# Decoder layer with mLSTM and routed experts: router by column groups ahead of the second projection, clears in the first turn, first feed-forward pair ahead of the last mLSTM transposes

## Chip, cores, metric

One core of a Trainium2 chip (trn2). The metric is the device time of one execution in microseconds, the median of several runs. All arithmetic is fp32 (TensorE operands too; some are split into an fp32r high and low part).

## What is computed

The input x is 16 sequences of 256 tokens with 512 features, beside a context of the same shape. Cut to what matters:

```python
x = layernorm(x + attention(x))            # 16 heads of 32, 4 key/value heads, rope on half of each head
x = layernorm(x + mlstm(q=x, k=ctx, v=ctx))  # 16 heads; two gates per head from [x, ctx, ctx]
logits = x @ router_w.T                    # 512 -> 16 experts
top2 = top_k(logits + router_bias, 2)      # weights: softmax scores of the two, made to sum to 1
out = sum over the two of weight * (silu(x @ Wu[e]) * (x @ Wg[e])) @ Wd[e]
out += (silu(x @ Su) * (x @ Sg)) @ Sd      # the shared expert, hidden width 512
return layernorm(x + out)
```

## The kernel before

`attention_and_mlstm` makes everything up to the router and the shared expert, one sequence (256 tokens, two tiles of 128) per turn; `experts` then runs 79 tiles of routed tokens, and `finish` normalises. The change touches the first function only.

**A turn is software-pipelined over three sequences**: `body(b, y, w, more)` holds attention of sequence b, the mLSTM of y=b-1, and router and shared expert of w=b-2. The turns are (0, -, -), (1, 0, -), then b=2 to 15 with all three, then (-, 15, 14) and (-, -, 15); b=3 to 14 are a hardware loop on VectorE and b=2 to 14 on the others. Each engine has its own instruction stream, written out by hand in an order of its own; the order between engines is set by semaphores alone (`wait(engine, signal, turn, count)`). Nothing is planned by a program.

**TensorE's order in a steady turn**: `qkv(0)`; transposes of x2 of w (`turn(x2T_ready, x2, 4)`, PSUM banks 4 and 5); transposes of x1 of y (banks 6 and 7); `qkv(1)` (L1111, 16 instructions for 8 matmuls, since an fp32 matmul is issued as two); `route()` (L1142: for both token tiles 4 matmuls that accumulate over the feature chunks, stationary x2T 128x128, moving router weights 128x16); `gate_mm()` (L1126, 24 matmuls of 256 columns); `ug(0)` of the shared expert (L1174, eight matmuls, su then sg); `turn_qk()` (L1161); `ug(1)`, `rank` (L1149 and L1150, which count the tokens chosen per expert), `ug(2)`, `ug(3)`; then the mLSTM's decay, score and sum matmuls over 16 heads with the scores of attention between them, then attention's second half, `down`, and the output projection (L1401). `ug(c)` for c of 2 and more waits for `hT_done` of pair c-2, which `hidden(c-2)` on VectorE gives (L865 and L870, behind `tanh(c-2)` on ScalarE, L571).

**ScalarE's order** there: `pass_through(0)` (L564), copy of x2T from PSUM (L578), x1T_hi (L583), `pass_through(1)`, Exp (L589) and Ln (L591) of the gates with a table load each time the function changes, qkT_hi (L597 and L600; this tile is also x1T_hi, so it waits for `mq_in`, the transfers that read it), then the tanh steps.

**VectorE's order**: `rope(0)`, x1T_lo (L926), `rope(1)` (L718 to L726), the router's top 2 (L935 to L947, small steps, each waiting for the one before), the gates (L955, then L957, which releases Exp, then L958), qkT_lo (L961 and L964), `hidden(0)`, two gate steps, `hidden(1)`, and so on.

**GpSimd's order**: `centre(y)` (L457 to L465), then, released by `gates_ready`, ctxT_hi (L488) and ctxT_lo (L490) of the next sequence, the key stack's 12 transfers, the routed ids' indirect transfers, and the stores. `clear_rows()` (four transfers that fill the id table and the spare rows, some 2.5 MB) comes between turn 0 and turn 1.

**SyncE** issues transfers: `mq_stack` from x1T (12), the next xT, `q_stack` from qkT (8 hi rows, 4 lo rows), the maxima, and `mk_stack` (12); at the start the constants (`first`), and after turn 0's maxima the six `late` loads, router weights and shared expert weights.

```python
def wait(eng, signal, b, n, rest=None):      # n-th step of turn b
def run(eng, body, then=None):               # the turns, in order
X_hi, X_lo = cast to fp32r, X - X_hi         # "hi" and "lo" rows of the stacks
```

Of the kernel before, what the change touches and what calls it, by code (L numbers as in the profile page):

```python
# [13 lines left out]
ALU = mybir.AluOpType  # L14
# [108 lines left out]
def attention_and_mlstm(nc, block, x, xT, ctx_in, ctxT, wqkv, wo, gate_w, gate_b, ln_scale, router_w, router_b,  # L123
# [3 lines left out]
    with ExitStack() as ctx:  # L127
# [23 lines left out]
        rw_sb = sb("rw_sb", [P, KC, E])  # L151
# [21 lines left out]
        mask_sb = arden[:, 0:P]  # L173
        ones_k = sb("ones_k", [P, HD])
# [76 lines left out]
        ps = ctx.enter_context(nc.psum_tensor("ps", [P, 8, 512], F32))  # L251
        ranks_of_turn = ps[:, 0, 0:2 * ST * E]
# [54 lines left out]
        lg_ready, lg_done = sig("lg_ready", 1), sig("lg_done", 1)  # L307
        top_step, choice_done = sig("top_step", 5 + TOPK), sig("choice_done", 1)
# [51 lines left out]
        def _(sp):  # L360
# [4 lines left out]
            late = [(rw_sb[:, :, :], router_w), (rb_sb[:, :], router_b.partition_broadcast(P)),  # L365
# [5 lines left out]
            sp.wait_ge(consts.sem, 1)  # L371
# [3 lines left out]
            def body(b, y, w, more):  # L375
# [9 lines left out]
                if b is not None:  # L385
# [3 lines left out]
                    wait(sp, qk_lo_done, b, 2)  # L389
                    stack(sp, q_stack, qkT_hi, qkT_lo, None, q_in, (None, None, "lo"))  # L390
                    if y is None:
                        sp.wait_ge(first_in.sem, 11 * 16)
                        sp.dma_start(wo_sb[:, :, :], wo).then_inc(first_in.sem, 16)
# [18 lines left out]
        def _(pool):  # L412
            rest = (pool.alloc_register("rest"), consts.sem)
            nc.gpsimd.memset(gb_sb[:, :], 0.0).then_inc(consts.sem, 1)
            nc.gpsimd.memset(one_col[:, :, :], 0.0).then_inc(fills.sem, 1)
# [52 lines left out]
            def body(b, y, w, more):  # L468
# [9 lines left out]
                if b is not None:  # L478
                    if y is None:
                        send_keys()  # L480
# [28 lines left out]
                if b is not None:  # L509
                    if y is not None:  # L510
                        wait(pool, av2_pair, y, PAIRS, rest=rest)
                    pool.dma_start(ctx_sb[:, :, :, :].rearrange("p t h d -> p t (h d)"), one(ctx_v, b)).then_inc(ctx_row_in.sem, 16)
                if y is not None:
# [23 lines left out]
            clear_rows()  # L537
# [10 lines left out]
        def _(act):  # L548
# [5 lines left out]
            def body(b, y, w, more):  # L554
# [24 lines left out]
                if y is not None:  # L579
# [3 lines left out]
                    nc.scalar.copy(x1T_hi[:, :, :], ps[:, 6:8, :].rearrange("p a (c s) -> p (a c) s", s=S))\  # L583
                        .then_inc(x1T_hi_done.sem, 1)
                if b is not None:
                    pass_through(1)
# [5 lines left out]
                if b is not None:  # L592
# [7 lines left out]
                    nc.scalar.copy(qkT_hi[:, KC, :], ps[:, 4, 0:S]).then_inc(qk_hi_done.sem, 1)  # L600
                def exp_gap():
# [88 lines left out]
        def _(dve):  # L690
# [4 lines left out]
            nc.vector.tensor_tensor(head_sel[:, :], id_sb[:, 0:H], id_sb[:, H:GR], ALU.add).then_inc(gwlo.sem, 1)  # L695
            nc.vector.tensor_reduce(is_lo[:, :], id_sb[0:GR, H:GR], AX.X, ALU.add).then_inc(gwlo.sem, 1)
# [1114 lines left out]
```

## Time and profile before

| | |
|---|---|
| median of 3 runs | 2015.57 us (2010.05 to 2018.85) |
| profiled execution, its own time | 2011.49 us |
| its span | 2009.9 us |
| mean granted TensorE clock | 0.962 of full |
| TensorE (PE) busy | 1834.2 us, 91% |
| VectorE (DVE) busy | 1141.7 us, 57% |
| GpSimd (POOL) busy | 690.4 us, 34% |
| ScalarE (ACT) busy | 644.1 us, 32% |
| chain that ended last | PE 78%, DVE 11%, issue 4%, ACT 3%, DMA 2% |

The sequences take the first 1475 us or so, the experts most of the rest. A busy TensorE need not be one at its peak: the times of its instructions include the pipeline's length, so their distance from start to start tells more than their duration.

### The profile page before, as it was taken

To read this page: it belongs to the slowest core of one execution; us is meant where nothing else is said; L and a number is where in the kernel's file an instruction comes from. 1 tells how busy PE (TensorE), PEld (TensorE's weight loads), DVE (VectorE), ACT (ScalarE), POOL (GpSimd) and SP (SyncE) were. 2 spreads that over 40 slices of the span, in tenths; PEclk is the share of its full clock that TensorE was granted. 3 is DMA by queue.
4 is the path that set the end of the run, shared out by engine and by line. 5 is a ranking of instruction groups with operands and counts; after the bars stand their busy time and mean duration, and the time that the engine had idled before them with its cause. 6 is when DMAs were issued, how large, how long until landed. Compare 5 with 4: busy or idle time off the path is not lost.

```text
span 2009.9 us, 35358 instructions
## 1 busy us (share of the span) xinstructions
PE 1834.2 (91%) x10992; PEld 1175.2 (58%) x10993; DVE 1141.7 (57%) x2407; ACT 644.1 (32%) x1355; POOL 690.4 (34%) x752
## 2 busy tenths in 40 slices
PE   5779999999999999999999999999789999999990
PEld 3456575766757676675766657576444544444440
DVE  3457776777677677766767677676432222222225
ACT  0242433424234252433434233352312211221124
POOL 3214233342323424233343323322224444444440
PEclk7889999999999999999999999998899999999995
DMA  5644243443424344242444424332416577656549
GB/s 160 190 112 113 58 109 83 102 118 69 123 63 102 103 94 127 49 123 74 98 112 89 123 63 102 90 79 73 147 43 134 109 202 168 120 119 145 92 76 342
DMA packets 151420, 225.94 MB, mean 112 GB/s; under 512 B 31888, under 2 KB 106640, under 8 KB 148816
## 3 DMA queue, kind: packets, MB, share of 16 engines
q1 hardware_dynamic: 102048, 132.94, 25.3%
q0 software_dynamic: 38112, 91.86, 20.2%
q10 hardware_dynamic: 11216, 0.61, 0.4%
q8 instruction: 22, 0.36, 0.1%
q14 instruction: 22, 0.18, 0.0%
HBM read 94.44 MB, written 48.57 MB: 71 GB/s over the span
## 4 chain that ended last, share of the span: by engine, by line
PE 78%; DVE 11%; issue 4%; ACT 3%; DMA 2%; SPq 1%; POOL 1%; DVEq 0%; ACTq 0%; POOLq 0%
PE ps L1621 14%; PE ps L1174 11%; PE ps L1111 8%; PE ps L1640 7%; PE ps L1401 6%; PE ps L1376 5%; PE ps L1260 5%; PE ps L1296 3%; PE ps L1365 3%; PE ps L1243 3%; DVE arden L912 3%; DVE smax L894 3%; PE ps L1126 2%; PE ps L1222 2%; PE ps L1609 2%
## 5 line engine op out<-in xcount | busy, mean ns | idle before, releaser
L1621 PE MATMUL ps<-ug_w,rowsT 128*128 x632 | 289.2, 601 | 7.9 <-SPq L1470 4.5
L502 POOL DMA_INDIRECT routed_ids<-pair_w,pos_w x64 | 64.0, 1000 | 446.3 <-DVE pair_w L790 431.7
L1621 PEld LDWEIGHTS ps<-ug_w,rowsT 128*128 128x128 f32 x632 | 121.4, 193 | 161.7 <-issue 161.7
L1510 POOL DMA_INDIRECT sum_rows<-y_sb,pairs x79 | 125.7, 1591 | 245.4 <-DVE y_sb L1588 126.6
L1111 PE MATMUL ps<-wqkv_sb,xT_sb 128*128 128x256 f32 (+1 forms) x512 | 172.6, 491 | 5.8 <-DMA wqkv_sb<-in_wqkv 5.8
L912 DVE RECIPROCAL arden<-ps 128x256 f32<-128x256 f32 x64 | 112.4, 1757 | 114.2 <-PE ps L1365 111.0
L1576 DVE SCALAR_TENSOR_TENSOR silu<-tanh,ps 128x256 f32<-128x256 f32 x79 | 33.2, 421 | 249.4 <-ACT tanh L1531 249.4
L1004 DVE SCALAR_TENSOR_TENSOR weighted<-ps,decay 128x384 f32<-128x384 f32 x256 | 140.2, 553 | 60.7 <-PE ps L1243 51.5
L894 DVE TENSOR_REDUCE smax<-ps 128x2 f32<-128x512 f32 x256 | 163.6, 680 | 13.4 <-PE ps L1296 13.4
L647 ACT ACTIVATE decay<-ps,g_col 128x256 f32<-128x256 f32 x256 | 121.3, 474 | 136.5 <-PE ps L1224 98.9
L1531 ACT ACTIVATE tanh<-ps 128x256 f32<-128x256 f32 x79 | 30.3, 384 | 370.7 <-PE ps L1621 370.7
L1640 PE MATMUL ps<-d_w,hidT 128*128 x316 | 148.6, 593 | 0.1
L668 ACT ACTIVATE probs<-ps 128x1024 f32<-128x1024 f32 x128 | 126.3, 1027 | 58.3 <-PE ps L1345 57.7
L1111 PEld LDWEIGHTS ps<-wqkv_sb,xT_sb 128*128 128x128 f32 x512 | 96.7, 192 | 80.5 <-issue 73.5
L1296 PE MATMUL ps<-k_stack,q_stack 96*128 96x256 f32 x512 | 112.8, 325 | 29.1 <-DMA q_stack<-qkT_lo 12.9
L564 ACT COPY hid_sq<-ps 128x320 f32<-128x320 f32 x32 | 13.6, 425 | 385.4 <-PE ps L1111 385.4
L1174 PE MATMUL ps<-x2T,su_sb 128*128 128x256 f32 x512 | 124.6, 387 | 1.9 <-DVE hT L870 1.6
L1401 PE MATMUL ps<-wo_sb,hid_sq 128*128 128x512 f32 x256 | 116.1, 607 | 5.5 <-DVE hid_sq L914 5.5
L1174 PE MATMUL ps<-x2T,sg_sb 128*128 128x256 f32 x512 | 121.0, 379 | 0.0
L515 POOL TENSOR_TENSOR hvar<-hvar,eps_half 128x32 f32<-128x32 f32 x16 | 87.4, 5464 | 87.2 <-DVE hvar L887 81.9
L1376 PE MATMUL ps<-sd_sb,hT 128*128 128x512 f32 x256 | 114.0, 598 | 0.7 <-DVE hT L870 0.7
L1260 PE MATMUL ps<-weighted,ctx_sb 128*32 128x256 f32 (+1 forms) x1024 | 108.6, 333 | 5.9 <-issue 5.5
(253 smaller groups left out, 3600.2 us busy)
## 6 DMA issues: line engine op xcount, KB each, us to landing
q_stack<-qkT_hi SPq DMA_DIRECT2D x128, 128.0 KB, 3.7
mk_stack<-ctxT_hi SPq DMA_DIRECT2D x128, 128.0 KB
mq_stack<-qkT_hi SPq DMA_DIRECT2D x128, 128.0 KB, 2.4
ug_w<-in_expert_ug SPq DMA_DIRECT2D x16, 1024.0 KB, 5.9
xT_sb<-in_xT SPq DMA_DIRECT2D x16, 512.0 KB, 3.4
q_stack<-qkT_lo SPq DMA_DIRECT2D x64, 128.0 KB, 4.9
x_sb<-in_x POOLq DMA_DIRECT2D x16, 512.0 KB, 3.9
ctxT_sb<-in_ctxT POOLq DMA_DIRECT2D x16, 512.0 KB, 3.8
```

Of the source, the lines that this page charges most:

```text
L668: nc.scalar.activation(probs[:, i % 4, :, :, :].rearrange("p j t s -> p (j t s)"), ps[:, 2 * (i % 2):2 * (i % 2) + 2, :].rearrange("p j n ...
L894: nc.vector.tensor_reduce(smax[:, k, :], ps[:, 3 + 4 * (k % 2), :].rearrange("p (t s) -> p t s", s=S), AX.X, ALU.max).then_inc(smax_done.s ...
L912: nc.vector.reciprocal(arden[:, :], ps[:, 6 + c % 2, cols]).then_inc(arden_done.sem, 1)
L1004: nc.vector.scalar_tensor_tensor(weighted[:, h % 4, :], ps[:, qk2_bank(h), 0:384], SCALE, decay[:, h % 2, :], ALU.mult, ALU.mult).then_inc ...
L1111: ins = nc.tensor.matmul(ps[:, 2 * t + lo // 512, 0:hi - lo], xT_sb[:, c, P * t:P * t + P], wqkv_sb[:, c, lo:hi], start=c == 0, stop=c == ...
L1174: ins = nc.tensor.matmul(ps[:, 6 + c % 2, lo:lo + S], wt[:, k, P * c:P * c + P], x2T[:, k, :], start=k == 0, stop=k == KC - 1)
L1260: nc.tensor.matmul(ps[lo:lo + HD, 4 + i // 4, col + cols.start:col + cols.stop], ctx_sb[:, t, h, :], weighted[:, h % 4, part], start=t == ...
L1296: ins = nc.tensor.matmul(ps[:, 3 + 4 * (k % 2), S * t:S * t + S], q_stack[0:96, k, P * t:P * t + P], k_stack[0:96, k // GQ, :], start=True ...
L1376: ins = nc.tensor.matmul(ps[:, 2 + t, :], hT[:, c, P * t:P * t + P], sd_sb[:, c, :], start=c == 0, stop=c == SC - 1)
L1401: ins = nc.tensor.matmul(ps[:, 6 + t, :], attT[:, c, P * t:P * t + P], wo_sb[:, c, :], start=c == 0, stop=c == KC - 1)
L1621: ins = nc.tensor.matmul(ps[:, 2 + k % 2, :], rowsT[:, k % 2, c, :], ug_w[:, bass.ds(slot, 1), c, :].rearrange("p o n -> p (o n)"), start= ...
L1640: ins = nc.tensor.matmul(ps[:, 4 + k % 2, :], hidT[:, k % 2, f, :], d_w[:, bass.ds(slot, 1), f, :].rearrange("p o d -> p (o d)"), start=f ...
```

## The change

1. **Router.** `route()` is split. `route_chunks()`, right ahead of `qkv(1)`, multiplies each chunk of router weights (128x32: 16 columns and 16 of zeros, hence a memset of rw_sb on GpSimd) as stationary with x2T's chunk as moving operand (256 columns), each chunk into its own 32 partitions of PSUM bank 4. ScalarE copies the 128x256 result to SBUF (into `arden`'s place). Behind `qkv(1)`, `route()` adds the four groups and transposes in one step: per token tile one matmul with the copied tile as stationary and `chunk_sum` (128x16) as moving operand. `route_chunks` waits for `x2T_done` before `qkv(1)`; before, that wait stood behind it.
2. **Clears.** `clear_rows()` moves into turn 0, behind the load of ctx_sb, and waits for the late loads first.
3. **First turn's stacks.** The key stack's hi rows go out as soon as hi is there, before lo; the query stack's lo rows go out from ScalarE's queue and not SyncE's.
4. **Turn (-, 15, 14).** `route_chunks()` and `ug(0)` come ahead of the transposes of x1, which go to banks 2 and 3 there.

```diff
-        rw_sb = sb("rw_sb", [P, KC, E])
+        rw_sb = sb("rw_sb", [P, KC, HD])
+        chunk_sum = sb("chunk_sum", [P, E])
+        lgT_sb = arden
+        X1_AT, X1_AT_LAST = 6, 2
...
 sync:
-            sp.wait_ge(consts.sem, 1)
+            sp.wait_ge(consts.sem, 2)
...
-                    wait(sp, qk_lo_done, b, 2)
-                    stack(sp, q_stack, qkT_hi, qkT_lo, None, q_in, (None, None, "lo"))
-                    if y is None:
+                    if y is not None:
+                        wait(sp, qk_lo_done, b, 2)
+                        stack(sp, q_stack, qkT_hi, qkT_lo, None, q_in, (None, None, "lo"))
+                    else:
...
 gpsimd:
+            nc.gpsimd.memset(rw_sb[:, :, :], 0.0).then_inc(consts.sem, 1)
...
                     if y is None:
-                        send_keys()
+                        wait(pool, qk_hi_done, b, 2)
+                        stack(pool, k_stack, qkT_hi, qkT_lo, KC, k_in, ("hi", None, "hi"))
+                        wait(pool, qk_lo_done, b, 2)
+                        stack(pool, k_stack, qkT_hi, qkT_lo, KC, k_in, (None, "lo", None))
...
                     pool.dma_start(ctx_sb[:, :, :, :].rearrange("p t h d -> p t (h d)"), one(ctx_v, b)).then_inc(ctx_row_in.sem, 16)
+                    if y is None:
+                        pool.wait_ge(late_in.sem, 6 * 16)
+                        clear_rows()
...
             body(0, None, None, True)
-            clear_rows()
             body(1, 0, None, True)
...
 scalar:
-                    nc.scalar.copy(x1T_hi[:, :, :], ps[:, 6:8, :].rearrange("p a (c s) -> p (a c) s", s=S))\
+                    at = X1_AT if b is not None else X1_AT_LAST
+                    nc.scalar.copy(x1T_hi[:, :, :], ps[:, at:at + 2, :].rearrange("p a (c s) -> p (a c) s", s=S))\
                         .then_inc(x1T_hi_done.sem, 1)
+                if w is not None:
+                    wait(act, lgT_ready, w, 1)
+                    nc.scalar.copy(lgT_sb[:, :], ps[:, 4, 0:S]).then_inc(lgT_done.sem, 1)
...
+                    if y is None:
+                        wait(act, qk_lo_done, b, 2)
+                        stack(act, q_stack, qkT_hi, qkT_lo, None, q_in, (None, None, "lo"))
...
 vector:
+            nc.vector.tensor_reduce(chunk_sum[:, :], id_sb[:, :].rearrange("p (j n) -> p n j", n=HD)[:, 0:E, :], AX.X, ALU.add)\
+                .then_inc(gwlo.sem, 1)
...
-                        lg = ps[:, 4, 0:ST * E].rearrange("p (t e) -> p t e", e=E)
+                        lg = ps[:, 4, S:S + ST * E].rearrange("p (t e) -> p t e", e=E)
...
 tensor:
+                def route_chunks():
+                    wait(pe, x2T_done, w, 1)
+                    for c in range(KC):
+                        ins = nc.tensor.matmul(ps[HD * c:HD * c + HD, 4, 0:S], rw_sb[:, c, :], x2T[:, c, :], start=True, stop=True)
+                    ins.then_inc(lgT_ready.sem, 1)
+
                 def route():
-                    wait(pe, x2T_done, w, 1)
+                    wait(pe, lgT_done, w, 1)
                     for t in range(ST):
-                        for c in range(KC):
-                            ins = nc.tensor.matmul(ps[:, 4, E * t:E * t + E], x2T[:, c, P * t:P * t + P], rw_sb[:, c, :],
-                                                   start=c == 0, stop=c == KC - 1)
+                        ins = nc.tensor.matmul(ps[:, 4, S + E * t:S + E * t + E], lgT_sb[:, P * t:P * t + P], chunk_sum[:, :],
+                                               start=True, stop=True)
...
+                ahead = b is None and y is not None
+                if ahead:
+                    route_chunks()
+                    wait(pe, h_done, y, 1)
+                    ug(0)
                 if y is not None:
                     wait(pe, x1_done, y, ST)
-                    turn(x1T_ready, x1, 6)
+                    turn(x1T_ready, x1, X1_AT_LAST if ahead else X1_AT)
+                if w is not None and not ahead:
+                    route_chunks()
...
-                if w is not None:
+                if w is not None and not ahead:
                     ug(0)
```

The counts of the semaphores consts and gwlo that others wait for grow by one each, and VectorE's x1T_lo reads the banks that x1T_hi reads.

## Rows read from the trace of the kernel before

**Rows 1.** TensorE in a steady turn, in order of time (start us, us, engine, line, operation).

```profile
432.03 5.33 PE L1111 MATMUL ps<-wqkv_sb,xT_sb 128*128 128x512 f32 x16
437.19 1.85 PE L1142 MATMUL ps<-rw_sb,x2T 128*128 128x16 f32 x16
438.90 0.31 PE L1126 MATMUL ps<-qkT_hi,gw_hi 128*64 128x256 f32 x1
...
441.75 1.89 PE L1174 MATMUL ps<-x2T,su_sb 128*128 128x256 f32 x8
...
449.89 0.39 PE L1150 MATMUL ps<-biased,ones_k 128*128 128x32 f32 x2
450.30 1.99 PE L1174 MATMUL ps<-x2T,su_sb 128*128 128x256 f32 x8
```

**Rows 2.** VectorE in the same turn, in order of time.

```profile
438.02 0.49 DVE L718 TENSOR_TENSOR hid_sq<-ps,cos_sb 128x320 f32<-128x320 f32 x1 [3.39 <-ACT v_sb L565]
...
441.43 0.49 DVE L944 TENSOR_TENSOR onehot<-choice,iota_sb 128x32 f32<-128x32 f32 x2
442.02 0.19 DVE L947 TENSOR_TENSOR biased<-onehot 128x32 f32<-128x32 f32 x1
...
442.63 0.92 DVE L957 SCALAR_TENSOR_TENSOR probs<-probs 32x256 f32<-32x256 f32 x1
443.48 2.43 DVE L958 TENSOR_SCALAR probs<-probs 32x256 f32<-32x256 f32 x1
...
449.82 0.42 DVE L870 SCALAR_TENSOR_TENSOR hT<-gate_sb,ps 128x256 f32<-128x256 f32 x1
```

**Rows 3.** ScalarE in the same turn; in brackets the idle time before and its end.

```profile
431.36 1.01 ACT L578 COPY x2T<-ps 128x1024 f32<-128x1024 f32 x1
...
446.35 1.01 ACT L597 CAST qkT_hi<-ps 128x1024 fp32r<-128x1024 f32 x1 [0.62 <-PE ps L1161]
```

**Rows 4.** Groups by line: TensorE's column-group form (busy us, mean ns, idle before).

```profile
L1365 PE MATMUL ps<-probs,v_sb 128*32 128x256 f32 x1024 | 81.2, 389 | 2.5 <-DVE hid_sq L914 1.2 <-ACT probs L668 0.4
```

**Rows 5.** GpSimd in the same steady turn, in order of time.

```profile
442.24 1.04 POOL L488 CAST ctxT_hi<-ctxT_sb 128x1024 fp32r<-128x1024 f32 x1 [3.00 <-PE ps L1126]
443.36 2.40 POOL L490 TENSOR_TENSOR ctxT_lo<-ctxT_sb,ctxT_hi 128x1024 fp32r<-128x1024 f32 x1
```

**Rows 6.** One line's instructions over all turns: ns least/median/most.

```profile
L957 DVE SCALAR_TENSOR_TENSOR probs<-probs x16: 414/924/1093, 95.0 to 1394.2; 32x256 f32<-32x256 f32 x16
...
L958 DVE TENSOR_SCALAR probs<-probs x16: 274/2431/2435, 95.8 to 1394.5; 32x256 f32<-32x256 f32 x16
```

**Rows 7.** TensorE behind idle times, in order of time, several stretches.

```profile
35.29 1.22 PE L1296 MATMUL ps<-k_stack,q_stack 96*128 96x256 f32 x4 [12.94 <-DMA q_stack<-qkT_lo]
...
71.59 3.68 PE L1401 MATMUL ps<-wo_sb,hid_sq 128*128 128x512 f32 x4 [2.93 <-DVE hid_sq L914]
...
156.86 8.83 PE L1401 MATMUL ps<-wo_sb,hid_sq 128*128 128x512 f32 x16 [2.61 <-DVE hid_sq L914]
...
1384.00 1.97 PE L1134 MATMUL ps<-id_sb,x 128*128 128x128 f32 x8 [4.83 <-DVE x L920]
...
1646.32 3.69 PE L1621 MATMUL ps<-ug_w,rowsT 128*128 x8 [2.23 <-SPq L1470]
```

**Rows 8.** SyncE's issues in turn 0, turn 1 and a steady turn.

```profile
53.38 0.43 SPq L401 DMA_DIRECT2D sd_sb<-in_sd  x1
...
88.94 9.29 SPq L354 DMA_DIRECT2D mq_stack<-qkT_hi  x8
...
434.81 5.11 SPq L354 DMA_DIRECT2D mq_stack<-qkT_hi  x8
```

**Rows 9.** ScalarE in turn 1.

```profile
106.05 1.01 ACT L597 CAST qkT_hi<-ps 128x1024 fp32r<-128x1024 f32 x1 [7.99 <-issue]
```

**Rows 10.** GpSimd at the end of turn 0.

```profile
82.67 0.56 POOL L530 TENSOR_SCALAR rstd<-mv 128x2 f32<-128x2 f32 x1 [35.37 <-DVE mv L1074]
```

**Rows 11.** Transfer issues by line (count, KB each, median us from issue to landing).

```profile
sd_sb<-in_sd SPq DMA_DIRECT2D x1, 1024.0 KB, 13.1
```

More of the change, by code:

```diff
@@ L307, in attention_and_mlstm @@
         lg_ready, lg_done = sig("lg_ready", 1), sig("lg_done", 1)
+        lgT_ready, lgT_done = sig("lgT_ready", 1), sig("lgT_done", 1)
         top_step, choice_done = sig("top_step", 5 + TOPK), sig("choice_done", 1)
@@ L364, in _ @@
                      (gb_sb[GR:GR + H, :], gate_b[1]), (gb_sb[GR + H:2 * GR, :], gate_b[1])]
-            late = [(rw_sb[:, :, :], router_w), (rb_sb[:, :], router_b.partition_broadcast(P)),
+            late = [(rw_sb[:, :, 0:E], router_w), (rb_sb[:, :], router_b.partition_broadcast(P)),
                     (lns_sb[:, :], ln_scale.partition_broadcast(P)),
@@ L699, in _ @@
             nc.vector.tensor_scalar(filled[:, :], iota_sb[:, 0:E], float(N), None, ALU.mult).then_inc(gwlo.sem, 1)
-            dve.wait_ge(gwlo.sem, 7)
+            dve.wait_ge(gwlo.sem, 8)
             nc.vector.tensor_scalar(row_p[:, :], row_p[:, :], -1.0, float(P - 1), ALU.mult, ALU.add).then_inc(gwlo.sem, 1)
             nc.vector.tensor_scalar(lo_sign[:, :], is_lo[:, :], 2.0, -1.0, ALU.mult, ALU.add).then_inc(gwlo.sem, 1)
-            dve.wait_ge(gwlo.sem, 9)
+            dve.wait_ge(gwlo.sem, 10)
             for t in range(ST):
                 nc.vector.tensor_scalar(token_f[:, t:t + 1], row_p[:, :], float(P * t), None, ALU.add).then_inc(gwlo.sem, 1)
-            dve.wait_ge(gwlo.sem, 11)
+            dve.wait_ge(gwlo.sem, 12)
             dve.wait_ge(pro.sem, 2 + GQ)
@@ L925, in front @@
                         wait(dve, x1T_hi_done, y, 1)
-                        nc.vector.tensor_tensor(x1T_lo[:, :, :], ps[:, 6:8, :].rearrange("p a (c s) -> p (a c) s", s=S),
+                        at = X1_AT if b is not None else X1_AT_LAST
+                        nc.vector.tensor_tensor(x1T_lo[:, :, :], ps[:, at:at + 2, :].rearrange("p a (c s) -> p (a c) s", s=S),
                                                 x1T_hi[:, :, :].bitcast(F32), ALU.subtract).then_inc(x1T_lo_done.sem, 1)
@@ L1119, in gate_mm @@
                     if w is None:
-                        pe.wait_ge(gwlo.sem, 12)
+                        pe.wait_ge(gwlo.sem, 13)
                         pe.wait_ge(late_in.sem, 6 * 16)
@@ L1199, in body @@
                         pe.wait_ge(first_in.sem, 11 * 16)
-                        pe.wait_ge(consts.sem, 3)
+                        pe.wait_ge(consts.sem, 4)
                     turn_qk()
```

## Prediction

> **What bounds it now.** The page has TensorE as by far the busiest engine, so the question is what each part does to the moments at which TensorE starts. I followed one steady turn (b=5) engine by engine; fourteen turns repeat it (b=2 to 15; two of them are written out around the loop, with somewhat shorter gaps between VectorE's small steps). Let T be 432.03, the start of the second projection, and Q be 437.19, its end, where the router starts [rows 1]. TensorE seems to run without a gap up to the rank matmuls, which end at 449.89+0.39=450.28. But ug(2) starts at 450.30, and what releases it is hT of pair 0, written by VectorE at 449.82+0.42=450.24 [rows 1, 2]. So **in each turn ug(2) is already tied to a second chain**, not to TensorE's amount of work. Read backwards it is: hidden(0) <- tanh(0) <- a table load <- the cast of qkT_hi (L597, 446.35) <- Ln <- another table load <- Exp <- VectorE's L957. In VectorE's order the router's top 2 and rope(1) stand in front of L957, and rope(1) begins at 438.02=Q+0.83 [rows 2, 3]. The one slack is the 0.62 us for which ScalarE waits for TensorE's transposes before L597 [rows 3].
>
> **The router in column groups (14 turns).** Removed: 16 instructions, 437.19 to 438.90, 1.71 us [rows 1]. Added:
> - Ahead of the projection a wait for x2T. ScalarE's copy ends at 431.36+1.01=432.37 [rows 3], TensorE is there at T; with some 0.03 for the signal 0.37 us. The whole projection is queued behind it.
> - Eight instructions of 256 columns in four 32-column groups. The same form in the attention sums has 81.2 us for 1024 instructions, 0.079 each beside its neighbours [rows 4]; 8x0.079=0.63 is the upper end. At four at once against the pace of ug's eight (1.89 [rows 1]) they take 1.89/4=0.47, which I take.
> - Behind the projection four instructions with the same 128x128 loads as the removed ones: 4x1.71/16=0.43. ScalarE's added copy (128x256) lies under the projection's 5.16 us, and would cost its own length without it.
>
> TensorE's own sum is 0.37+0.47+0.43-1.71=-0.44 us a turn. But the projection now ends at Q'=Q+0.84, everything on the second chain moves with it, and the gate matmuls end 1.71-0.43=1.28 us nearer to Q'.
>
> **What that triggers on GpSimd.** GpSimd casts ctxT (L488) when the gate matmuls are done, Q+5.05 to Q+6.09, then subtracts (L490), Q+6.17 to Q+8.57 [rows 5]. VectorE's L957 takes 0.41 at its least and 0.92 here: it ends at 443.55, 0.27 behind L488's end. L958 takes 0.27 at its least and 2.43 here, to 445.91, 0.15 behind L490's end [rows 2, 5, 6]. Both stand still until the GpSimd instruction is over; today the long one falls on L958, for which nobody hurries. After the change L488 runs from Q'+3.77 to 4.81 and L490 from Q'+4.89 to 7.29. VectorE is where it was against Q': the two L944 at +4.24 and about +4.5, L947 at +4.83, L957 at +5.44 [rows 2]. **L490 now falls on the critical ones.** The first L944 waits for L488; the second, or L947, meets L490 and waits to Q'+7.3; L957 follows 0.61 behind L947 as today and ends at Q'+8.3 to 8.7, against Q+6.36. Lower bound: L957 alone is held, 7.29+0.27=7.56, +1.20. Upper: +2.39. I take +2.10 in the twelve looped turns (L957 is the nearest row: the same partner, two operands in SBUF) and +1.2 in the two others, where the small steps come earlier. Less the slack of 0.62, ug(2) starts 0.84+2.10-0.62=2.32 us later than today, or 1.42. Nothing behind gives it back: hidden(2) and with it the decay matmuls hang on ug(2). Sum 12x2.32+2x1.42=**+30.7 us**; bounds 14x1.42=20 and 14x2.61=37.
>
> A rule bears on the race between the second L944 and L490. The Trainium skill (SBUF — State Buffer, "SBUF: two separate sides") says that whichever of the two starts first keeps the shared ports for its whole instruction. By that rule a second L944 that starts in the gap before L490 passes, L947 is held in its place, and the sum is some 12x0.25=3 us lower. The rows show the lock, but not who wins a start this close.
>
> **The clock.** Rank's matmuls would end at about Q'+11.8, ug(2) starts at Q'+14.6: TensorE idles 2.8 us in each turn. Behind 2.93 us of idling four L1401 took 3.68; behind 2.61 sixteen took 8.83, where the projection's pace (5.16 for the equal of twelve) gives 6.9, so 1.9 lost; that is the pace of 1.2 in place of 2.4 GHz for a while. Behind 2.23 eight matmuls took 3.69, with nothing lost to see [rows 1, 7]. A gap of 2.8 is nearest the first two but will come in varied phases: I take two turns in three at 1.75, 14x2/3x1.75=**+16.3 us**; bounds 0 and 14x1.9=27.
>
> **First turn.** The stacks' hi rows go out without waiting for lo, and q's lo rows by ScalarE's queue. The first scores start at 35.29, after 12.94 us of waiting for q's lo rows [rows 7]. SyncE issues 8 transfers in place of 12 (5.11/8=0.64 each [rows 8]), 2.6 less, but GpSimd's twelve key transfers are then the last to land: **-2.1**, bounds 0 and -2.6. ScalarE is idle there. One more memset ahead of SyncE's constants and one small reduction lie beside its earlier issues and the first loads; uncovered, under 1 us.
>
> **Clears.** In turn 1 eight mq_stack transfers take 9.29 us against 5.11 in a steady turn, beside the clears, and L597 waits 7.99 us, to 106.05, for the stack to have read its source [rows 8, 9]. With the clears gone twelve go out in 7.7 us from 88.94 and land some 2.4 later, at 99.1: **-6.9**; bounds 0 (the contention has another source) and -8. In turn 0 GpSimd now waits for the late weights, with rstd1 queued behind it. It is idle for 35.37 us up to 82.67 [rows 10]; the last of the weights is issued at 53.38 and lands 13.1 later, at 66.5 [rows 8, 11], and four issues follow. Hidden; if the weights came past 80, the delay would be direct.
>
> **Last two turns.** TensorE waits 4.83 us for x1 [rows 7]. ug(0), some 3.5 us (twice rows 1's eight), now runs in it, and the half pace behind it (1.97 for the eight transposes) goes: **-4.0**, bounds -3.4 and -6. In the very last turn the shorter router gives **-0.7**, bounds 0 and -1.7.
>
> **Sum.** 30.7+16.3-2.1-6.9-4.0-0.7=+33.3. The profiled execution took 2011.5 us (span 2009.9), 0.2% under the median of 2015.6; 2011.5+33.3=2045. What can be told from no change is about 0.5%, 10 us.
>
> **Rivals.**
> - *The lock bites at L957 only, the clock stays up*: 20-14=+6, 2018. For: the small steps move only 32 elements, and a gap of 1.9 us is below the 2.23 that cost nothing. Against: their operands lie as L957's. 0.14.
> - *No collision, faster.* The place is L957's start. If L488 starts at least 1.1 us later than the gates' end lets it (released by something else than the row's TensorE wait), L490 falls on L958 again: 14x(0.84-0.62)-14=-11, 2001. If ug(2) was tied to TensorE alone after all, -0.44x14-14=-20, 1991. For: the release is inferred. Against: the row names the gate matmuls. 0.13 together.
> - *Worst bounds*: 37+27-10=+54, 2066. 0.06.
> - *The groups don't run together* (the change doesn't do what it says): 1.72 in place of 0.47, 14x1.25=17 more, 2062. 0.02; rows 4 speak against it. The Trainium skill (TensorE: Matmul & The Clock Gate, "Part 3: Packing small matmuls") has weight loads overlap running matmuls only where the row group differs; here all share one. By that rule this rival is the truth; the trace disagrees.
>
> **Numbers.** The forecast keeps 0.65, with a range of its own from 2026 (little of the clock's term) to 2062. The range 2010 to 2062 leaves out the fast case and the worst. Slower than 2025.6: 0.71; within 0.5%: 0.17; faster: 0.12.
>
> **What would show it.** Right: in steady turns a wait of TensorE for L870's hT of 2.5 to 3 us, where none is listed; L944 or L947 stretched past 1.5 us; L958 back near 0.27; a granted clock below 1.00 in steady turns; the chunks in 0.43 to 0.63; L597's wait in turn 1 down from 7.99 to about 1; x1's 4.83 gone. Wrong: L957 ending before Q'+7, or ug(2) no later than T+18.3.

## The result, and the profile after

The changed kernel takes **2068.02 us** (median of 4 runs, 2059.82 to 2074.11) against 2016.89 us for the kernel before, run beside it on the same chip (4 runs). The ratio is **1.0257, with an interval of 1.0210 to 1.0304**. The forecast was 2045 us with a range of 2010 to 2062: the direction was right, the size too small, and the median lies outside the range.

The profiled execution took 2059.82 us: a span of 2058.3 us at a mean granted clock of 0.954, against 2009.9 at 0.962. All that follows compares these two spans, so there are 48.4 us to find where the forecast had 33.3. The first lines of the page after, with the chain that ended last:

```profile
span 2058.3 us, 35249 instructions
...
PE 1844.8 (90%) x10928; PEld 1168.2 (57%) x10929; DVE 1144.1 (56%) x2408; ACT 647.2 (31%) x1371; POOL 689.4 (33%) x753
...
PE 68%; DVE 16%; ACT 7%; issue 5%; DMA 2%; SPq 1%; POOL 1%; DVEq 0%; ACTq 0%; POOLq 0%
```

Hardly any engine has more work. What changed is the chain: TensorE's share fell from 78% to 68%, VectorE's rose from 11% to 16% and ScalarE's from 3% to 7%. TensorE's list of waits says where the chain now leaves TensorE (engine, line, what it waited for: us in total, times, longest):

```profile
PE ps L1200 <- DVE hT L890: 43.4, 16, 2.9
PE ps L1329 <- DMA q_stack<-qkT_hi: 15.2, 1, 15.2
...
PE ps L1342 <- DVE probs L1001: 8.4, 1, 8.4
```

The wait of ug(2) for VectorE's hT was not listed for steady turns before; now it comes in all fourteen of them, 2.90 or 2.91 us in the twelve looped ones and 2.4 in the two written out. Here is one steady turn. The numbers of the lines have moved: L1132, L1147, L1187, L1200, L963, L965, L968, L978, L979, L890, L612, L497 and L499 are what L1111, L1126, L1161, L1174, L942, L944, L947, L957, L958, L870, L597, L488 and L490 were. TensorE in order of time, to be laid beside [rows 1]:

```profile
1070.18 0.64 PE L1162 MATMUL ps<-x2T,rw_sb 128*32 128x256 f32 x8 [0.23 <-ACT x2T L589]
1070.75 5.43 PE L1132 MATMUL ps<-wqkv_sb,xT_sb 128*128 128x512 f32 x16
1076.01 0.52 PE L1168 MATMUL ps<-chunk_sum,arden 128*128 128x16 f32 x4
1076.38 0.31 PE L1147 MATMUL ps<-qkT_hi,gw_hi 128*64 128x256 f32 x1
...
1087.33 0.39 PE L1176 MATMUL ps<-biased,ones_k 128*128 128x32 f32 x2
1090.62 3.78 PE L1200 MATMUL ps<-x2T,su_sb 128*128 128x256 f32 x8 [2.91 <-DVE hT L890]
```

Q' is 1076.01. From the first of the eight chunk instructions to the projection behind them it is 0.57 us, and the join takes 0.37. Rank's matmuls are over at 1087.72, ug(2) starts at 1090.62, Q'+14.61, and its eight instructions take 3.78 us instead of 1.89: they run at 1.2 GHz, not 2.4. VectorE in the same turn, beside [rows 2]:

```profile
1079.88 0.86 DVE L963 CAST choice<-top8i 128x4 f32<-128x4 uint32 x1
1080.85 2.65 DVE L965 TENSOR_TENSOR onehot<-choice,iota_sb 128x32 f32<-128x32 f32 x2
1083.61 0.19 DVE L968 TENSOR_TENSOR biased<-onehot 128x32 f32<-128x32 f32 x1
...
1084.22 0.41 DVE L978 SCALAR_TENSOR_TENSOR probs<-probs 32x256 f32<-32x256 f32 x1
1084.56 0.27 DVE L979 TENSOR_SCALAR probs<-probs 32x256 f32<-32x256 f32 x1
...
1090.15 0.42 DVE L890 SCALAR_TENSOR_TENSOR hT<-gate_sb,ps 128x256 f32<-128x256 f32 x1
```

And GpSimd, beside [rows 5]:

```profile
1079.68 1.04 POOL L497 CAST ctxT_hi<-ctxT_sb 128x1024 fp32r<-128x1024 f32 x1 [2.70 <-PE ps L1147]
1080.80 2.36 POOL L499 TENSOR_TENSOR ctxT_lo<-ctxT_sb,ctxT_hi 128x1024 fp32r<-128x1024 f32 x1
```

Put the ends side by side. The cast of four numbers per partition, L963, ends at 1080.74, right after GpSimd's cast ends at 1080.72. L965 is issued at 1080.85, 0.05 us behind the start of GpSimd's subtraction; the two L965 take 2.65 us together instead of 0.49, and the first of them ends only when the subtraction is over (1083.16). L978 and L979, which were stretched before [rows 6], are now at their least, 0.41 and 0.27. So GpSimd's long instruction has moved from an instruction that nobody waits for to one at the head of the critical chain. Over all turns it shows in the duration of these lines (ns least/median/most). L965 stands there twice a turn and only one of the two is held, so its median is the free one; L979 is now free in nearly every turn:

```profile
L965 DVE TENSOR_TENSOR onehot<-choice,iota_sb x32: 191/193/2356, 176.0 to 1503.6; 128x32 f32<-128x32 f32 x32
```

```profile
L979 DVE TENSOR_SCALAR probs<-probs x16: 274/274/2419, 96.5 to 1442.7; 32x256 f32<-32x256 f32 x16
```

The clock, by turn (window, its length, then busy time of each engine, granted clock, DMA share, GB/s). The three rows are a turn with one fall, one without, and one of the late ones:

```profile
432.13:523.15 91.02, 85.06 (x596) 58.03 (x595) 61.51 (x128) 32.65 (x69) 29.58 (x35) 0.98 0.38 92
523.15:612.47 89.32, 83.38 (x596) 56.83 (x595) 61.51 (x128) 32.64 (x68) 29.57 (x35) 1.00 0.40 92
...
1069.12:1161.23 92.11, 86.14 (x596) 58.81 (x595) 61.45 (x128) 32.64 (x68) 29.57 (x35) 0.96 0.37 89
```

and a turn of the kernel before in the same view:

```profile
431.36:518.05 86.69, 83.86 (x600) 58.00 (x599) 61.33 (x128) 32.47 (x68) 29.67 (x35) 1.00 0.41 96
```

So a looped turn costs 89.3 us where the clock stays at 2.4 GHz, 2.63 more than before. With a part of it at 1.2 GHz it is 91.0 (granted clock 0.98) or 92.1 (0.96). Five of the fourteen stay at full clock, two looped ones and the last lose some 1.7 us each, and six in a row, from 793 us on, lose 2.8 each. The two prices come from two lengths of the slow stretch, here one of each (windows set to its ends):

```profile
454.72:458.15 3.43, 3.43 (x10) 2.72 (x9) 2.26 (x5) 0.00 (x0) 3.43 (x8) 0.50 0.94 214
905.29:912.12 6.83, 5.76 (x14) 4.60 (x15) 4.10 (x9) 0.49 (x2) 5.93 (x12) 0.50 0.99 213
```

In the first the granted clock is at half for 3.43 us, all of them behind the start of ug(2) at 453.70; half of that is the 1.7 us. In the second it is at half for 6.83 us and already from 1.07 us before ug(2) starts; TensorE works in 5.76 of them, and half of those is the 2.8.

### The profile page after: what moved, and what is told of

It reads as the page before. It is cut to its first block, busy times and chain, and to the rows that moved or that the text cites. A ratio compares the mean times of both kernels' runs of the same rounds, so it can differ in the third digit from the quotient of the medians.

```text
span 2058.3 us, 35249 instructions
## 1 busy us (share of the span) xinstructions
PE 1844.8 (90%) x10928; PEld 1168.2 (57%) x10929; DVE 1144.1 (56%) x2408; ACT 647.2 (31%) x1371; POOL 689.4 (33%) x753
## 4 chain that ended last, share of the span: by engine, by line
PE 68%; DVE 16%; ACT 7%; issue 5%; DMA 2%; SPq 1%; POOL 1%; DVEq 0%; ACTq 0%; POOLq 0%
PE ps L1654 13%; PE ps L1132 8%; PE ps L1200 7%; PE ps L1673 7%; PE ps L1434 5%; PE ps L1409 5%; PE ps L1293 4%; PE ps L1329 3%; PE ps L1398 3%; DVE arden L932 3%; PE ps L1276 3%; DVE smax L914 3%; PE ps L1255 2%; DVE onehot L965 2%; PE ps L1642 2%
## 5 line engine op out<-in xcount | busy, mean ns | idle before, releaser
L1132 PE MATMUL ps<-wqkv_sb,xT_sb 128*128 128x256 f32 (+1 forms) x512 | 174.4, 494 | 5.9 <-DMA wqkv_sb<-in_wqkv 5.9
L1200 PE MATMUL ps<-x2T,su_sb 128*128 128x256 f32 x512 | 140.1, 422 | 43.4 <-DVE hT L890 43.4
L1609 DVE SCALAR_TENSOR_TENSOR silu<-tanh,ps 128x256 f32<-128x256 f32 x79 | 33.3, 421 | 250.0 <-ACT tanh L1564 250.0
L1132 PEld LDWEIGHTS ps<-wqkv_sb,xT_sb 128*128 128x128 f32 x512 | 96.8, 192 | 86.6 <-issue 79.1
L1200 PEld LDWEIGHTS ps<-x2T,su_sb 128*128 128x128 f32 x512 | 103.7, 210 | 60.5 <-DVE hT L890 45.8
L1200 PE MATMUL ps<-x2T,sg_sb 128*128 128x256 f32 x512 | 130.1, 400 | 0.0
L1200 PEld LDWEIGHTS ps<-x2T,sg_sb 128*128 128x128 f32 x512 | 105.3, 206 | 17.1
```

The source lines that it names most:

```text
L1132: ins = nc.tensor.matmul(ps[:, 2 * t + lo // 512, 0:hi - lo], xT_sb[:, c, P * t:P * t + P], wqkv_sb[:, c, lo:hi], start=c == 0, stop=c == ...
L1200: ins = nc.tensor.matmul(ps[:, 6 + c % 2, lo:lo + S], wt[:, k, P * c:P * c + P], x2T[:, k, :], start=k == 0, stop=k == KC - 1)
```

## The experiments

The theory (T): the release of GpSimd's casts by the gate matmuls comes 1.3 us nearer to Q', so its subtraction holds VectorE's top-2 steps and with them hT; the 2.9 us for which TensorE then waits let its clock fall. Rivals: the router's new work or its new wait costs the time by itself; another part of the change does; the clock's fall has a source of its own. All kernels were timed against the kernel before on their own chip: the first four below on one, the delayed gate matmuls and the old router with later casts on a second, the three parts and the last version on a third. Between chips, and against the changed kernel's own 2068.02, the ratios are the fairer measure. Each kernel has one trace, so what is read from a trace is one execution.

### Starting GpSimd's casts later

```diff
 gpsimd, in the changed kernel, ahead of the cast of ctxT (L497):
                         wait(pool, gates_ready, y, 1)
+                        wait(pool, gabs_done, y, 1)
```

> The changed kernel with one wait more: GpSimd starts the two ctxT instructions (L488 and L490 of before) only when VectorE's L957 (|forget gate|) is done. Port theory: L957 then ends near Q'+5.8 instead of Q'+8.6, the wait for hT ahead of ug(2), 2.9 us in each steady turn, shrinks under 0.3 us, the clock stays at 2.4 GHz in the steady turns, and the time is about 2007 us (before 2017, less 9 of the first and last turns, about 0 in the steady ones). Rival, the chain is long for another reason (rope moved back, ScalarE's extra copy): the wait stays near 2 to 3 us and the time near 2068.

Measured: **1999.27 us** (1998.57 to 2002.41), before 2011.83, ratio 0.9943 [0.9926, 0.9960]. One wait more, on an engine that is a third busy, takes 69 us off the changed kernel by the medians (63 by the two ratios; the kernel before ran 5 us slower on the changed kernel's chip). The expectation was 2007: 5 us of the miss are the chip's, since it reckoned from 2017, and 4 come from the fourteen turns, which are shorter than those of the kernel before (1203.4 us together against 1207.5) where nothing had been expected. VectorE in a steady turn of it (all numbers of lines are one higher):

```profile
954.92 0.17 DVE L964 CAST choice<-top8i 128x4 f32<-128x4 uint32 x1
955.19 0.49 DVE L966 TENSOR_TENSOR onehot<-choice,iota_sb 128x32 f32<-128x32 f32 x2
...
956.40 0.41 DVE L979 SCALAR_TENSOR_TENSOR probs<-probs 32x256 f32<-32x256 f32 x1
956.74 0.27 DVE L980 TENSOR_SCALAR probs<-probs 32x256 f32<-32x256 f32 x1
...
962.33 0.42 DVE L891 SCALAR_TENSOR_TENSOR hT<-gate_sb,ps 128x256 f32<-128x256 f32 x1
```

GpSimd's cast there, and behind it TensorE around ug(2):

```profile
957.17 1.04 POOL L498 CAST ctxT_hi<-ctxT_sb 128x1024 fp32r<-128x1024 f32 x1 [5.13 <-DVE probs L979]
958.29 2.36 POOL L500 TENSOR_TENSOR ctxT_lo<-ctxT_sb,ctxT_hi 128x1024 fp32r<-128x1024 f32 x1
```

```profile
962.37 0.39 PE L1177 MATMUL ps<-biased,ones_k 128*128 128x32 f32 x2
962.80 1.99 PE L1201 MATMUL ps<-x2T,su_sb 128*128 128x256 f32 x8
```

Nothing on VectorE is held any more, L979 ends 5.8 us behind the second projection's end as expected, ug(2) follows rank with no wait listed, and the turn takes 86.42 us at full clock:

```profile
512.08:598.50 86.42, 83.31 (x596) 56.74 (x595) 58.64 (x128) 32.65 (x69) 29.64 (x35) 1.00 0.43 96
```

### The old router in the changed kernel

```diff
 tensor:
-                def route_chunks(): ...
                 def route():
-                    wait(pe, lgT_done, w, 1)
+                    wait(pe, x2T_done, w, 1)
                     for t in range(ST):
+                        for c in range(KC):   # the sixteen instructions of before
 scalar:
-                    nc.scalar.copy(lgT_sb[:, :], ps[:, 4, 0:S]).then_inc(lgT_done.sem, 1)
```

> The changed kernel with the old router (8 accumulating matmuls behind the second projection, no copy on ScalarE); clears, first stacks and the early ug(0) stay. If all of the loss is the router's: 2017-9=2008, steady turns back at 86.7 us. If one of the other parts also costs: above 2020.

Measured: 2001.64 us (2000.36 to 2003.59), ratio 0.9948 [0.9931, 0.9965]. Clears, stacks and the ug pair ahead are thus worth about 10 us together, and everything that the change costs is in the router. The 2008 expected reckoned from 2017 as well.

### The new router alone

```diff
 the changed kernel, router as changed; back to before:
+            clear_rows()   # behind body(0, None, None, True)
+                        send_keys()
-                ahead = b is None and y is not None
+                ahead = False
-        X1_AT, X1_AT_LAST = 6, 2
+        X1_AT, X1_AT_LAST = 6, 6
```

> The router's part alone: clears, first stacks and the turn (-, 15, 14) as before. If the parts add up: the changed kernel's 2068 plus the 9 us that the other parts gave, 2077. If the other parts gave nothing, 2068.

Measured: **2078.19 us** (2072.90 to 2086.52), ratio 1.0335 [1.0301, 1.0369]. As expected (2077), the router costs 66 us by itself, and in company the same: 66 by the medians of changed kernel and old router (2068.02 and 2001.64), 62 by their ratios. The full wait and the falls are there, in TensorE's waits and in one turn's window. In its trace twelve of the fourteen turns have a fall, ten of them in a row at the higher price:

```profile
PE ps L1191 <- DVE hT L881: 41.2, 15, 2.9
```

```profile
604.00:696.10 92.10, 86.17 (x598) 58.84 (x594) 61.40 (x128) 32.61 (x68) 29.53 (x36) 0.96 0.36 90
```

### Filling TensorE's wait

```diff
 tensor, in the changed kernel, behind rank in steady turns:
                             rank(ranks_of_turn)
+                            if b is not None:
+                                for _ in range(6):
+                                    nc.tensor.matmul(ps[:, 1, 0:S], su_sb[:, 0, 0:P], x2T[:, 0, :], start=True, stop=True)
```

The six matmuls compute nothing that is used. They do not shorten the wait for hT; they only keep TensorE at work in it, so they take the clock's part away and leave the lock's (the lock: VectorE's steps standing still until GpSimd's instruction ends).

> The changed kernel with six needless matmuls (256 columns, 2.6 us at full clock, result not used) behind rank in each steady turn, in the gap of 2.9 us. Clock theory: TensorE never idles, the clock stays up in the steady turns, each turn takes 89.3 us as those of the changed kernel without a fall, and the time drops by 20 to 30 us, to about 2043. Rival, the lower clock costs nothing beyond the wait: the same 2068, or a little more.

Measured: **2037.37 us** (2036.58 to 2038.81), ratio 1.0129 [1.0112, 1.0146]. TensorE at ug(2):

```profile
538.63 2.84 PE L1243 MATMUL ps<-x2T,su_sb 128*128 128x256 f32 x12
541.69 1.99 PE L1200 MATMUL ps<-x2T,su_sb 128*128 128x256 f32 x8 [0.22 <-DVE hT L890]
```

and a whole turn:

```profile
520.17:609.47 89.30, 86.05 (x608) 58.96 (x607) 61.50 (x128) 32.61 (x69) 29.57 (x35) 1.00 0.40 92
```

ug(2) is as late as ever (the turn is 89.30), but it starts at 2.4 GHz. So of what lies between the changed kernel and the one with the later casts, **38 us are the lock's (2037.37 - 1999.27, both from one chip) and 31 the clock's by the medians (2068.02 - 2037.37), 26 by the ratios, 22 by the two profiled spans (2058.3 - 2035.8)**. The 38 agree with the turns: 12 x (89.30 - 86.42) is 34.6, and the first and the last steady turn bring some 4 more. The runs also scatter over 2.2 us, where the changed kernel's scatter over 14. One of the fourteen turns still has a fall, of 1.1 us, but in another place: some 33 us into the turn, among the mLSTM's matmuls, behind waits of 0.35 and 0.38 us. Such single falls of 1.1 us, where there is no wait of 2.9, stand in the traces of five of the experiments (one to three each) and in none of the kernel before or the changed one, so a small part of the clock's loss has a source of its own, which no run here looks into.

### Moving the gate matmuls back by needless work

The first two experiments changed the router or a wait. This one keeps both as in the changed kernel and only delays the gate matmuls' end, by 1.28 us of matmuls whose result is not used.

```diff
 tensor, in the changed kernel:
                     route()
+                    if b is not None:
+                        for _ in range(3):
+                            nc.tensor.matmul(ps[:, 5, S:2 * S], su_sb[:, 0, 0:P], x2T[:, 0, :], start=True, stop=True)
                 if y is not None:
                     gate_mm()
```

> The changed kernel with three needless matmuls (256 columns, 1.28 us) between route and the gate matmuls, which puts GpSimd's two instructions back to where they stood against VectorE in the kernel before. Port theory: L490 falls on L958 again, L957 ends at Q'+6.4, TensorE no longer idles ahead of ug(2) and the clock stays up: a turn of 87.7 us, 1999.3+14x(87.7-86.4)=2018, 50 us less than the changed kernel although TensorE does more. Rival, the loss comes from the later projection and the split router: 2068 plus 14x1.28=2086.

Measured: **2018.55 us** (2015.98 to 2021.0, 10 runs), before 2013.47, ratio 1.0025 [1.0014, 1.0036]. Work added to the engine with the longest busy time makes the kernel nearly 50 us faster (2068.02 - 2018.55; 47 by the ratios). VectorE's rows are back to the pattern of before [rows 2]:

```profile
878.39 1.05 DVE L978 SCALAR_TENSOR_TENSOR probs<-probs 32x256 f32<-32x256 f32 x1
879.37 2.44 DVE L979 TENSOR_SCALAR probs<-probs 32x256 f32<-32x256 f32 x1
```

and the clock stays up in eleven of the fourteen turns. The looped ones take 87.7 to 87.8 us, as expected, except three with a fall of 1.1 us among the mLSTM's matmuls. The new router, its wait for x2T and its copy are all still there, so the rival that they cost the time falls. What decides is where GpSimd's pair stands against VectorE's small steps.

### The old router with the later casts

The edits of the first two experiments together.

> e2_old_router with GpSimd's later start of e1_pool_later: what is the column-group router worth once the port collision is away? Steady turns of e2 are 86.65 us and those of e1 86.41. If the later start alone gives nothing here (L957 0.5 us shorter, but ug(2) tied to TensorE's transposes and the tanh chain): 2001.6, so the router is worth 2 to 3 us. If it gives all: 1999 or less.

Measured: 2003.44 us (2000.83 to 2005.09), ratio 0.9953 [0.9940, 0.9966], against 0.9943 [0.9926, 0.9960] with the column-group router and the same late casts. The turns take 86.64 and 86.42 us: 14 x 0.22 = 3 us is what the new router is worth once nothing collides. The runs agree with that, but their intervals overlap. It is also the control for the first experiment: with the old router the later casts give nothing (0.9953 against 0.9948 without them), so the 63 to 69 us are not something that a later GpSimd would have given anyway.

### What the other parts are worth

Each of these takes the kernel with the later casts (1999.27 us, ratio 0.9943) and puts one part back to what it was. They ran on another chip than it did, with the kernel before at nearly the same time (2011.65 and 2011.83).

```diff
 clears back in their old place:
             body(0, None, None, True)
+            clear_rows()
```

> On top of e1_pool_later (1999.3 us, steady turns undisturbed) the clears go back between turn 0 and turn 1. By the contention theory ScalarE's L597 in turn 1 waits some 7 us again, and TensorE's wait for the gate columns goes from 8.4 back to about 16: 1999.3+7=2006. If the clears' place is worth nothing: 1999.

Measured: 2005.15 us (2001.6 to 2008.16, 11 runs), ratio 0.9966 [0.9956, 0.9976]: the clears are worth 6 us by the medians, 5 by the ratios. In the traces ScalarE's wait ahead of the cast in turn 1 is 5.69 us instead of 1.03, and TensorE's wait for the gate columns 13.1 instead of 8.4 (not 16, as expected), so 4.7 us by either.

```diff
 stacks back: lo rows of q behind the hi rows on SyncE, keys by
+                        send_keys()
```

> On top of e1_pool_later the first turn's stacks go back (keys after lo, q's lo rows on SyncE's queue). I had forecast 2.1 us for this part, but TensorE's first wait for the stacks is 13.5 us there against 12.9 in the kernel before: the part is worth nothing or costs a little. Forecast 1999; if it is worth what I first said, 2001.4.

Measured: 2000.45 us (1998.36 to 2005.77), ratio 0.9948 [0.9933, 0.9963]: 1.2 us, which can't be told from nothing.

```diff
 no ug pair ahead, x1 transposed into banks 6 and 7 as before:
-                ahead = b is None and y is not None
+                ahead = False
```

> On top of e1_pool_later the turn (-, 15, 14) goes back to transposes of x1 first, ug(0) behind the gates. First forecast of this part 4.0 us, and the distance between the last two x2T copies gives 2.3 (67.9 against 70.3): 2001.6 to 2003.3. If nothing: 1999.3.

Measured: 2004.37 us (2000.19 to 2007.17), ratio 0.9957 [0.9941, 0.9973]: by the medians the pair ahead would be worth 5 us, by the ratios 3, and the intervals overlap. The traces give some 2.5: from the copy of x2T in that turn to the one in the next it is 69.2 to 70.4 us in the three kernels without the pair ahead and 66.2 to 69.5 in the nine with it (medians 70.3 and 67.8). Much of the rest has nothing to do with this part: in the profiled execution 2.9 of the 8.0 us by which it is longer stand in front of the first steady turn. The three parts add up to 12.2 by the medians and 8.4 by the ratios, against 10.2 in the old router's run.

### A version that beats both

With GpSimd out of the way, hT's chain starts with the gates' columns, which wait behind the top 2 on VectorE and behind the router on TensorE. This version, on top of the later casts, puts the gates first on both.

```diff
 tensor:
-                    route_chunks()          # ahead of qkv(1)
                     qkv(1)
-                    route()
+                    route_chunks()
                     gate_mm()
+                    route()
 vector: the three steps on gates and forget (L976 to L979) ahead of the top 2 (from L956)
 scalar: the copy to lgT_sb behind pass_through(1)
```

> On top of e1_pool_later: route_chunks goes behind the second projection, route behind the gate matmuls, ScalarE's copy of the chunk sums behind pass_through(1), and VectorE does the gates (L955 to L958) ahead of the router's top 2. If ug(2) is tied to the chain rope(1) - top 2 - gates - Exp, it then starts at about Q+12.4 against Q+13.1 in the kernel before and T+5.2 against T+6.2 for Q: 0.6 to 0.8 us less in each of 14 turns than e1, 1989 to 1991. If TensorE's own amount of work is the limit already: 1998 to 2000. If VectorE's L958 or the top 2 now meets GpSimd's instructions on a path that matters, slower than 2005.

Measured: **1993.32 us** (1987.55 to 1999.60, 5 runs), before 2011.65, **ratio 0.9900 [0.9884, 0.9917]**: 1% faster than the kernel before and 3.5% faster than the changed one, though 2 us short of the 1989 to 1991 expected. A turn takes 86.07 us in its trace, 0.35 less than with the later casts alone, where 0.6 to 0.8 was expected. VectorE and ScalarE in a steady turn show what binds it next:

```profile
957.29 0.41 DVE L957 SCALAR_TENSOR_TENSOR probs<-probs 32x256 f32<-32x256 f32 x1
...
959.69 1.86 DVE L971 CAST choice<-top8i 128x4 f32<-128x4 uint32 x1
...
965.10 0.42 DVE L891 SCALAR_TENSOR_TENSOR hT<-gate_sb,ps 128x256 f32<-128x256 f32 x1
```

```profile
961.63 1.01 ACT L613 CAST qkT_hi<-ps 128x1024 fp32r<-128x1024 f32 x1 [1.75 <-PE ps L1188]
```

The subtraction now holds the top 2's cast (1.86 us), where nobody waits. The gates' chain has become so early that ScalarE waits 1.75 us for TensorE's transposes before L613, so the chain behind hT now starts at the transposes, and what the gates gained above that is lost. ug(2) starts at 965.57, 0.05 behind hT's end at 965.52: it is still tied to hT.

## Why the prediction was right in its mechanism and wrong in its size

**The collision: right, to a tenth of a microsecond.** Q'+8.3 to 8.7 was forecast for the end of L957 (now L978); it came at 1084.22+0.41 = Q'+8.62. ug(2) at Q'+14.6: Q'+14.61. An idle time of 2.8 us ahead of it: 2.91. The run with delayed gate matmuls shows that this coincidence, and not the router's own time, is what costs. Only the steps that are held are one earlier than forecast: the text took the first L944 to meet L488 and the second L944 or L947 to meet L490, but the cast L942 already met L488, and the first L944 met L490. That is still the forecast's upper side.

The rule weighed there (the Trainium skill, SBUF — State Buffer, "SBUF: two separate sides": whichever starts first keeps the shared ports for its whole instruction) agrees with the rows: the first L965 was issued 0.05 us behind L499 and waited for all of it. The case in which the rule would have saved 3 us, a small step that starts just ahead of L490 in the looped turns, did not arise there. It did in the first steady turn, where the gaps between the small steps are smaller: the second L965 ended at 177.25 (175.98+1.27), so it had begun about when the subtraction did, and L968 was held in its place, which fits the rule.

```profile
175.98 1.27 DVE L965 TENSOR_TENSOR onehot<-choice,iota_sb 128x32 f32<-128x32 f32 x2
177.28 2.23 DVE L968 TENSOR_TENSOR biased<-onehot 128x32 f32<-128x32 f32 x1
```

```profile
177.06 2.40 POOL L499 TENSOR_TENSOR ctxT_lo<-ctxT_sb,ctxT_hi 128x1024 fp32r<-128x1024 f32 x1
```

**The lock's term: 30.7 forecast, 35.3 measured.** By the turns at full clock it is 1.9 in the first steady turn, 12 x 2.63 and 1.86 in the last. The forecast had 2.32 and 1.42. Of the 0.31 a turn, 0.23 is the router itself: Q' comes 6.23 us behind T where the text had 6.00, because the chunks take 0.57 us and not 0.47, the wait for x2T 0.40 and not 0.37, and the projection behind them 5.26 and not 5.16. Taking the chunks as four at once at the full pace was too kind; the row for the attention sums [rows 4] gave 0.63. The 1.2 us for the two written-out turns was the other mistake: there L978 ended at Q'+8.10 and Q'+8.07, which is 1.7 and 1.9 later than its like before, since the steps were held until GpSimd's end all the same.

**The clock's term is the step that failed: 16.3 forecast, some 22 measured in the profiled executions, and 26 to 31 by ratios and medians.** The number of turns was right (two in three was taken, nine of fourteen had a fall), but by luck: no row stood behind the two in three, and with the router alone it was twelve of fourteen. The price was wrong. The text took 1.75 us for each, from the two rows behind 2.93 and 2.61 us of idling [rows 7]. Three turns lost 1.7; six lost 2.8, because TensorE there worked at 1.2 GHz for 5.76 us and not for 3.43. The trace of the kernel before already had a longer stretch than those two rows: around the 4.83 us of waiting for x1 [rows 7] the granted clock is at half from 1382.4 to 1392.6. 3 x 1.7 + 6 x 2.8 is 22, and with the 35.3 of the lock gives the 57.4 us by which the fourteen turns grew (1207.45 to 1264.87 us, from the copy of x2T for b=2 to that of the last). The upper bound of 27, fourteen times 1.9, was no bound: it let every turn fall but none for longer than the one example.

The changed kernel's runs spread from 2060 to 2074, and the longer they are, the lower their mean granted clock (0.954, 0.952, 0.947 and 0.946), so the falls differ from run to run; the profiled execution was the fastest. Of the 23 us between 2045 and 2068, 15 are what the two profiled executions show. The other 8 are the distance of the changed kernel's median from its profiled execution, and of these 5 would have been there in any case: the text added its sum to a profiled execution of 2011.5, and the kernel before has a median of 2016.89.

Why six turns in a row fall for longer, while earlier ones with the same wait (2.90 or 2.91 us) don't or don't at all, is **open**: no run here separates it. In the terms of the sum the profiled execution lies 15.1 us above the forecast: 5.8 by the clock, 4.6 by the lock, 2.6 by the first turns and 2.1 by the last.

**The first turns: -9.0 forecast, -6.4 measured.** The clears' part is as told. TensorE's wait for the gate columns was 15.9 us before and is 8.4 now. L597 (now L612) is hardly held any more, and SyncE's eight transfers take 5.11 us in turn 1, not 9.29 [rows 8, 9]; SyncE's row and ScalarE's:

```profile
89.67 5.11 SPq L358 DMA_DIRECT2D mq_stack<-qkT_hi  x8
```

```profile
99.29 1.01 ACT L612 CAST qkT_hi<-ps 128x1024 fp32r<-128x1024 f32 x1 [0.55 <-issue]
```

With the clears put back, 5 to 6 us returned where 6.9 was forecast. The stacks' part failed: the first scores come 3.8 us later, not 2.1 earlier. 1.6 of these lie before the wait for the stacks begins, and differ as much between other traces (it begins at 21.4 to 25.4 us in all twelve). The last to land are now q's hi rows, which nothing had been expected of:

```profile
39.10 1.22 PE L1329 MATMUL ps<-k_stack,q_stack 96*128 96x256 f32 x4 [15.16 <-DMA q_stack<-qkT_hi]
```

The wait was 12.94 us before [rows 7] and 12.9 and 13.0 in the two experiments without this part; with it it is 15.16 here and 12.4 to 16.5 in the others. SyncE's own row has the reason nearest at hand: with three queues sending at once, its eight issues of q's hi rows took 7.93 us in the first turn, against 5.31 for the same eight before.

```profile
24.86 7.93 SPq L358 DMA_DIRECT2D q_stack<-qkT_hi  x8
```

In the nine traces with this part the eight issues take 6.5 to 8.2 us, in the three without it 5.3, and the wait grows with them (6.49 with 12.4, 8.16 with 16.5). The text had taken issue times from a steady turn and saved on their number; spread over three queues each became longer. By the run without this part it costs or gives nothing that can be told from none.

**The last turns: -4.7 forecast, -2.6 measured.** The 4.83 us of waiting for x1 is gone. In its place come smaller waits, in TensorE's rows of that turn:

```profile
1431.29 0.64 PE L1162 MATMUL ps<-x2T,rw_sb 128*32 128x256 f32 x8 [1.10 <-ACT x2T L589]
...
1437.83 0.62 PE L1168 MATMUL ps<-chunk_sum,arden 128*128 128x16 f32 x4 [1.38 <-ACT arden L599]
...
1447.67 3.48 PE L1200 MATMUL ps<-x2T,su_sb 128*128 128x256 f32 x8 [2.04 <-DVE hT L890]
```

There is no second projection in that turn, so ScalarE's copy (arden, L599) has no cover, as the text had said of the general case without applying it here; and behind the wait for hT TensorE runs at 1.2 GHz for a while. By the traces the pair ahead is worth some 2.5 us and not 4.0: these waits were put at nothing.

**The rivals.** That the groups don't run together (2062) was close in the total and wrong in its cause: eight instructions took 0.57 us, a third of what that rival needs. The Trainium skill (TensorE: Matmul & The Clock Gate, "Part 3: Packing small matmuls") allows weight loads to overlap running matmuls only where row groups differ; the trace disagrees here too, for its loads, all of one row group, did not lengthen the chunks to one after the other. That section of the Trainium skill has matmuls in different column groups run together all the same, three of them 2.38 times as fast, and the trace agrees: four took 0.57 us, where eight instructions of full width take 1.72, three times as fast. The fast rival named its own deciding point rightly: with L488 at least 1.1 us later than the gates' end lets it, it gave 2001, and the run with the later casts measured 1999.27. The case that both bounds come at once (2066) was given 0.06 and is nearest in its total, though neither term reached its bound in the profiled execution (35.3 against 37, 22 against 27).

By the sum: 35.3 + 22.1 - 6.4 - 2.6 = 48.4, the difference of the spans.

## What to carry to other kernels

Before work on one engine is shortened, look at what its end releases elsewhere: a GpSimd instruction released 1.3 us earlier landed on VectorE's critical small steps in every turn and cost more than the whole change could save, and one wait that puts it behind them took the loss away. If a change puts a wait of two or three microseconds on TensorE into every turn of a loop, price the clock by the longest slow stretch in the trace and not by the nearest example, and test with needless matmuls in the gap: they tell the clock's part from the wait's in one run. And a wait in a part without the usual neighbour (first or last turn) has to be costed without the cover that neighbour gives.

## What the hardware showed that was not expected

- **Size doesn't protect a VectorE instruction from GpSimd's.** A cast of four numbers per partition from uint32, 0.17 us by itself, took 0.86 us beside GpSimd's cast and 1.86 beside its subtraction, in each case until GpSimd's instruction ended.
- **The same idle time costs the clock differently.** With 2.9 us of idling in every turn, turns lost nothing, 1.7 us or 2.8 us, the last six times in a row (ten times in the router-only kernel); with the idling cut to 0.22 us by needless matmuls none lost anything there.
- **Needless work on the busiest engine made the kernel faster** in two places: by 47 to 50 us with 1.28 us of it a turn ahead of the gate matmuls, by 26 to 31 us with 2.6 us a turn (12 x 0.214) behind rank.
- **Three queues did not land the stacks sooner than two**: the first scores waited for 12.4 to 16.5 us with the split (nine traces) and 12.9 to 13.0 without (three), and SyncE's eight issues took 6.5 to 8.2 us instead of 5.3.
